# First mixer pass of a sandwich layer: x loaded ahead, the first of two row sums on GpSimd, the sums ahead of the scan, u by ScalarE

## What is computed

```python
x = x + 0.5 * _L0_ffn_ref(_layernorm(x, axis=-1), Wg, W11, W12, W2)      # 8 experts, 2 chosen per row
x = x + _L0_attn_ref(_layernorm(x, axis=-1), ...)                        # the mixer
x = x + 0.5 * _L0_ffn_ref(_layernorm(x, axis=-1), Wg, W11, W12, W2)
```

```python
rms = jnp.sqrt(jnp.mean(T * T, axis=-1, keepdims=True) + EPS)
x, z = jnp.split(T / rms * norm_scale @ in_w.T + in_b, 2, axis=-1)
gate = jax.nn.sigmoid(z)
xc = conv over 3 rows of x, per channel, + dw_b;  xc = xc @ pw_w.T + pw_b
u = xc @ win.T                              # 64 states, once forward, once backward
h = h * Abar + u_t * Bbar;  y_t = h * C     # a scan along the 4096 rows
y = (y_f @ wout_f.T + y_b @ wout_b.T) * gate
return T + y @ out_w.T + out_b
```

## Time and profile before

| | us |
|---|---|
| median of three runs (1027.65 to 1031.73) | 1029.53 |
| the profiled execution, by the clock of the runs | 1027.42 |
| its span in the profile | 1025.7 |
| TensorE busy in the span | 913.5 (89%) |
| VectorE busy | 603.9 (59%) |
| GpSimd busy | 547.1 (53%) |
| ScalarE busy | 356.7 (35%) |
| the first mixer pass lies at about | 431 to 546 |

### The profile page before, as it was taken

The page is one execution under the profiler, slowest core; times in us unless marked ns, Lnnn a source line. Parts: engine busy times, 40 slices in busy tenths (PEclk is TensorE's granted clock), DMA queues, the critical chain, the costliest instruction groups (busy, mean ns, idle before and its releaser), DMA issues.

```text
span 1025.7 us, 19076 instructions
## 1 busy us (share of the span) xinstructions
PE 913.5 (89%) x5386; PEld 784.5 (76%) x5390; DVE 603.9 (59%) x1456; ACT 356.7 (35%) x684; POOL 547.1 (53%) x565
## 2 busy tenths in 40 slices
PE   7669999999999999847787994599999999999994
PEld 7658888888888888726665784488888888888883
DVE  3976566565575655555655884755555555555552
ACT  3644344344343333223324531033333333333331
POOL 3435566565665555223212540166777677777762
PEclk9989999999999999958899995699999999999998
DMA  9653534525525421266511558133343333333322
GB/s 315 209 164 119 196 104 144 194 84 162 178 74 197 137 85 48 80 200 223 165 61 61 185 174 343 48 79 73 52 77 77 51 72 58 75 72 56 56 42 27
DMA packets 83903, 123.58 MB, mean 120 GB/s; under 512 B 12656, under 2 KB 64496, under 8 KB 83600
## 3 DMA queue, kind: packets, MB, share of 16 engines
q1 hardware_dynamic: 45344, 59.98, 17.6%
q0 software_dynamic: 24992, 37.32, 16.7%
q10 hardware_dynamic: 13520, 25.70, 7.5%
HBM read 74.67 MB, written 48.30 MB: 120 GB/s over the span
## 4 chain that ended last, share of the span: by engine, by line
PE 64%; DVE 14%; issue 8%; DMA 4%; POOL 4%; ACT 3%; ACTq 1%; another core or an unknown queue 1%; SPq 0%; POOLq 0%; DVEq 0%
PE bank L1493 34%; PE bank L1516 18%; PE bank L1502 5%; PE bank L1485 3%; DMA seq<-y_rows 2%; PE bank L1614 1%; DMA seq<-xt 1%; DVE bnst L878 1%; DVE work L1223 1%; POOL rstd L475 1%; POOL seq L502 1%; DVE work L1221 1%; DVE w_lo L1231 1%; ACT work L771 1%
## 5 line engine op out<-in xcount | busy, mean ns | idle before, releaser
L1163 DVE TENSOR_TENSOR sg<-sg,bank 128x512 f32<-128x512 f32 x142 | 97.7, 688 | 278.3 <-ACT sg L700 199.9
L1493 PE MATMUL bank<-w_hi,xt_hi 128*128 x568 | 238.0, 419 | 10.7 <-DVE xt_lo L1152 9.6
L1493 PE MATMUL bank<-w_hi,xt_lo 128*128 x568 | 223.8, 394 | 0.0
L1493 PE MATMUL bank<-w_lo,xt_hi 128*128 x568 | 223.5, 394 | 0.0
L511 POOL DMA_INDIRECT xg<-xn_rows,idx_i x142 | 140.5, 989 | 100.0 <-DVE idx_i L1001 42.0
L692 ACT ACTIVATE yb<-bank,gates_in 128x256 f32<-128x256 f32 x142 | 67.5, 475 | 306.6 <-PE bank L1516 257.6
L1516 PE MATMUL bank<-w_hi,ft_hi 128*128 x568 | 160.2, 282 | 2.2 <-ACT yb L692 2.2
L515 POOL DMA_INDIRECT gates_in<-gate_rows,idx_g x142 | 135.9, 957 | 47.7 <-issue 42.7
L1516 PE MATMUL bank<-w_lo,ft_hi 128*128 x568 | 160.4, 282 | 0.0
L1516 PE MATMUL bank<-w_hi,ft_lo 128*128 x568 | 160.2, 282 | 0.0
L525 POOL DMA_INDIRECT out_rows<-yb,idx_i x71 | 115.0, 1620 | 61.8 <-ACT yb L692 27.9
(11 more groups left out here) (268 smaller groups left out, 1256.5 us busy)
## 6 DMA issues: line engine op xcount, KB each, us to landing
w_lo_rows<-w_lo ACTq DMA_DIRECT2D x16, 512.0 KB
w_lo<-w_lo_rows SPq DMA_DIRECT2D x16, 512.0 KB
w_lo<-w_lo_rows SPq DMA_DIRECT2D x2, 4096.0 KB, 17.3
xn_rows<-work SPq DMA_DIRECT2D x14, 512.0 KB, 3.1
x_all<-x SPq DMA_DIRECT2D x8, 512.0 KB, 10.2
w_lo_rows<-in_sb ACTq DMA_DIRECT2D x16, 256.0 KB
work<-x SPq DMA_DIRECT2D x8, 512.0 KB, 3.4
states<-y_rows SPq DMA_DIRECT2D x8, 512.0 KB, 4.2
```

The source lines that it names most:

```text
L1163: nc.vector.tensor_tensor(sg[p], sg[p], ps_g[p][:], ALU.mult).then_inc(f_step, 1)
L1493: last = nc.tensor.matmul(dst[p][:], xt[p][:, c, :], of(w), start=(c == 0 and n == 0), stop=(c == DC - 1 and n == len(parts) - 1))
```

## The change

It has these parts, all in the first mixer pass:

1. x is not loaded chunk by chunk into `xin`. All of it goes to `x_place`, the places of `gate` where the gates of the same chunk will be written later: twelve half chunks as soon as the experts' weights have left that memory, the other four after the mixer's folded matrices are ready.
2. y has three buffer pairs, in `seq` and in `states` with `in_sb`. y of chunks 0 and 1 is loaded at once, y of chunk 2 after the matrices, and y of chunk i+2 when chunk i is summed (i from 1).
3. GpSimd adds the second choice's rows to the first (`sum_choices`), one chunk ahead of its `rsqrt_rms`. VectorE adds x and that sum, one addition where there were two.
4. VectorE does the sums and statistics of chunk c+4 ahead of the scan of chunk c.
5. u is taken by ScalarE (with a bias column `UBIAS` made beforehand), between the high parts and the gates.
6. The loops of ScalarE and VectorE are written out; zeros for the edge columns come from another place; TensorE's first filler matmuls wait for the first sum instead of the first x.

```diff
         xn_x = [xn[0], xn[1], states[:].rearrange("p a n -> p (a n)").rearrange("p (t d) -> p t d", d=D)]
-        y_in_sb = [states[:].rearrange("p a n -> p (a n)"), seq[:, 0, 3080:3080 + G * D]]
+        x_place = [gate[:, :, k * CH:(k + 1) * CH] for k in range(NCH)]
+        y_place = [[seq[:, 0, 8:8 + G * D], seq[:, 0, 8 + G * D:8 + 2 * G * D]],
+                   [seq[:, 0, 8 + 2 * G * D:8 + 3 * G * D], seq[:, 0, 8 + 3 * G * D:8 + 4 * G * D]],
+                   [states[:].rearrange("p a n -> p (a n)"), in_sb[:].rearrange("p a n -> p (a n)")]]
+        y_buffer = [0, 1, 2, 1, 2, 1, 2, 1]
...
+            sp.wait_ge(lo_out, 32 * E)
+            for i in range(NCH):
+                for h in range(2 if i < NCH // 2 else 1):
+                    load_x(i, h, x_early)
             for p in range(2):
                 sp.wait_ge(y_out[p], 16 * ((ET + 1 - p) // 2))
-            sp.wait_ge(lo_out, 32 * E)
-            load_x1(0, 0)
             load_y(0)
-            load_x1(1, 1)
+            load_y(1)
+            sp.wait_ge(m_ready, 1)
+            load_y(2)
+            for i in range(NCH // 2, NCH):
+                load_x(i, 1, x_late)
             for i in range(NCH):
                 b = i % 2
                 sp.wait_ge(summed, i + 1)
-                if i + 1 < NCH:
-                    load_y(i + 1)
+                if 1 <= i < NCH - 2:
+                    load_y(i + 2)
                 sp.dma_start(rows(x1_dram, i), xin[b]).then_inc(x1_out[b], 16)
-                if i + 2 < NCH:
-                    sp.wait_ge(norm_ready, i + 1)
-                    sp.wait_ge(x1_out[b], 16 * (i // 2 + 1))
-                    load_x1(i + 2, b)
...
+            def sum_choices(i):
+
+                first, second = y_place[y_buffer[i]]
+                pool.wait_ge(y_in[y_buffer[i]], 32 * y_buffer[0:i + 1].count(y_buffer[i]))
+                nc.gpsimd.tensor_tensor(first, first, second, ALU.add).then_inc(half_sum, 1)
+
+            sum_choices(0)
             for i in range(NCH):
+                if i + 1 < NCH:
+                    sum_choices(i + 1)
                 rsqrt_rms(i, i % 2)
...
+            def take_u(c, b):
+
+                act.wait_ge(u_done, c + 1)
+                if c >= NCH // 2:
+                    act.wait_ge(summed, NCH)
+                nc.scalar.activation(seq[:, 0, c * CH + 1:(c + 1) * CH + 1], ps_u1[b][:], ACT.Identity, scale=ssm[:, BBAR:BBAR + 1], bias=ssm[:, UBIAS:UBIAS + 1]).then_inc(u_ready, 1)
...
+            def stats_x1(i, b):
+                x_rows, y_rows = x_place[i], y_place[y_buffer[i]]
...
+                if i >= 2:
+                    dve.wait_ge(x1_out[b], 16 * (i // 2))
+                    dve.wait_ge(norm_ready, i - 1)
                 dve.wait_ge(half_sum, i + 1)
-                nc.vector.tensor_tensor(flat, flat, y_in_sb[1], ALU.add).then_inc(summed, 1)
+                halves = lambda a: a.rearrange("p (h n) -> p h n", h=2)
+                whole_ = xin[b].rearrange("p t d -> p (t d)")
+                nc.vector.tensor_tensor(halves(whole_), x_rows, halves(y_rows[0]), ALU.add).then_inc(summed, 1)
                 dve.wait_ge(summed, i + 1)
                 ln_stats(i + NCH, b, rows_of(b))
```

More of the change, by code:

```diff
@@ L262, in build @@
         xn_x_out = [sem(f"xn_x_out{b}") for b in range(3)]
+        y_in = [sem(f"y_in{b}") for b in range(3)]
         y_out = [sem(f"y_out{b}") for b in range(2)]
-        y_in, half_sum, summed, norm_dve, norm_act, r_ready = (sem(n) for n in ("y_in", "half_sum", "summed", "norm_dve", "norm_act", "r_ready"))
+        x_early, x_late, half_sum, summed, norm_dve, norm_act, r_ready = (sem(n) for n in ("x_early", "x_late", "half_sum", "summed", "norm_dve", "norm_act", "r_ready"))
         x_in = [sem(f"x_in{b}") for b in range(2)]
@@ L780, in _ @@
             norm_x1(3, 1)
-            with act.Fori(0, NCH // 2 - 2) as j:
-                for b in range(2):
-                    rows_high(j * 2 + (b + 2), b)
-                    gate_out(j * 2 + (b + 1))
-                    norm_x1(j * 2 + (b + 4), b)
-            for i in range(NCH - 2, NCH):
-                rows_high(i, i % 2)
-                gate_out(i - 1)
-            gate_out(NCH - 1)
+            for c in range(NCH):
+                if c + 2 < NCH:
+                    rows_high(c + 2, c % 2)
+                take_u(c, c % 2)
+                if c + 1 < NCH:
+                    gate_out(c + 1)
+                if c + 4 < NCH:
+                    norm_x1(c + 4, c % 2)
             def take_states(i, b, c):
@@ L1286, in _ @@
             for b in range(2):
-                stats_x1(b, 0, b)
+                stats_x1(b, b)
             dve.wait_ge(m_ready, 1)
@@ L1290, in _ @@
             rows_low(0, 0)
-            stats_x1(2, 1, 0)
+            stats_x1(2, 0)
             rows_low(1, 1)
-            stats_x1(3, 1, 1)
-            with dve.Fori(0, NCH // 2 - 2) as j:
-                for b in range(2):
-                    c = j * 2 + b
-                    take_u(c, b)
-                    rows_low(j * 2 + (b + 2), b)
-                    scan_forward(c)
-                    stats_x1(j * 2 + (b + 4), j + 2, b)
-            nc.vector.memset(states[N:P, 1, 0:1], 0.0).then_inc(bwd_done, 1)
-            for c in range(NCH - 4, NCH):
-                take_u(c, c % 2)
-                if c < NCH - 2:
-                    rows_low(c + 2, c % 2, last=(c == NCH - 3))
-                scan_forward(c)
+            stats_x1(3, 1)
+            for c in range(NCH):
+                if c + 2 < NCH:
+                    rows_low(c + 2, c % 2, last=(c == NCH - 3))
+                if c + 4 < NCH:
+                    stats_x1(c + 4, c % 2)
+                scan_forward(c)
+            nc.vector.memset(states[N:P, 1, 0:1], 0.0).then_inc(bwd_done, 1)
             def scan_backward(i, b):
@@ L1635, in _ @@
             pe.wait_ge(m_ready, 1)
-            pe.wait_ge(x_in[0], 16)
+            pe.wait_ge(summed, 1)
             keep_busy(ps_t1[1][0][:], before.unsqueeze(1).to_broadcast([P, G, P]), 12)
```

35 lines of the change are left out of this document (17 added, 18 removed).

## The result

The changed kernel takes 1023.66 us in the median of eleven runs (1018.82 to 1026.26), the kernel before 1029.53 (1026.92 to 1032.83). The ratio is 0.9939, with a 95% interval of 0.9922 to 0.9956: 6.3 us less by it (4.5 to 8.0), 5.9 by the medians. The prediction was 1024.2. The profiled execution of the changed kernel has a span of 1022.1 us against 1025.7, 3.6 less.

What follows compares the result with a forecast made beforehand. The first pass was taken to be bound by a loop of latencies among VectorE, GpSimd and ScalarE, no engine full. Start -3.2, three loops -4.1 and end +2.05 gave -5.3 us: 1024.2 from 1029.53, range 1021 to 1028.

Steps and rivals of the forecast that it cites:

- The loop: Steady chunk of the first pass: falls from 12.36 to 10.98 us, 1.38 less.
- The scan's 1.19 and the add's 1.23: Steady chunk: moving the scan and giving one add to GpSimd take 1.19 and 1.23 us off VectorE's chain.
- The block: Steady chunk: the scan, now beside GpSimd's small rstd steps, holds them up and costs 1.04 us.
- The rival in which GpSimd gets through: Steady chunk: scan does not hold GpSimd up, loop 9.94 us, total -11.0, 1018.5 us; chance 0.15.
- The start: First chunks of the pass: low halves of chunk 2 come 1.8 us earlier, of chunk 3 3.2 us.
- TensorE's first product: Start: u of chunk 0 ready at 472.3 us; evacuation of chunk 2 waits for it, low halves follow at 473.4.
- x ahead: Start: early x loads cost nothing, and y of chunk 0, first in the queue, comes 1.4 us earlier.
- The end: Hand-over to the second pass: last u, scan and two hand-offs stand before the states' copy, 2.05 us more.
- The sum: Whole kernel: -3.2 start, -4.1 chunks 4 to 6, +2.05 end, -5.3 us; median 1024.2 us.
- the start gains nothing and new meetings of adds take half of each loop's gain: Start and steady chunks: only -0.8 us in total, 1028.8 us; chance 0.20.
- the rival of the late load: Steady chunk: y landing after 7.3 us makes GpSimd's sum delay VectorE's add; up to +4.3, 1033.8 us; chance 0.06.
- TensorE at half clock in the whole pass: First pass: clock sinks to 1.2 GHz, TensorE becomes the loop, +20 us with the end, 1049 us; chance 0.04.

Runs made afterwards that it cites:

- scan behind rstd: Changed kernel, with the scans of chunks 0 to 3 also waiting for GpSimd's rstd; ratio to the kernel before 0.9900.
- last kernel: Changed kernel with u before gates, scan behind rstd, first product ahead of chunk 2's transposes, ten fillers, and both adds of chunks 0 and 1 on VectorE; ratio 0.9823.
- kernel of the mends and fillers: Changed kernel with u before gates, scan behind rstd, first product ahead of chunk 2's transposes, and ten filler products behind the last gates; ratio 0.9835.
- product first kernel: Changed kernel, with TensorE's 36 products for u of chunk 0 ahead of the transposes of chunk 2; ratio to the kernel before 0.9918.
- u before gates: Changed kernel, with ScalarE taking u of the last chunk ahead of the last chunk's gates; ratio to the kernel before 0.9906.
- u on VectorE: Changed kernel with one part undone: VectorE takes u again, ahead of the low halves; ratio to the kernel before 0.9903.

## Why the prediction was right

**The loop.** Forecast 10.98, measured 10.82. The scan's 1.19 and the add's 1.23 left it as written. The block was sized at 1.04 from the earlier trace rows and measured 0.87: the first step took 1.10, and it had been 0.23, not 0.20. Undoing one part each gave 12.08 (add back) and 9.96 (block away), and moving the scan alone in the kernel before gave 12.08 instead of 12.37, which is 1.19 off and 0.90 back. So all three terms are shown.

**The block by the scan.** The rival in which GpSimd gets through is refuted by the scan behind rstd: same scan, same GpSimd steps, other place. The rule of the Trainium skill (SBUF — State Buffer, "Who interferes with whom"), that a VectorE instruction with two inputs in SBUF and a GpSimd instruction that reads SBUF exclude each other, holds in these runs for adds too where VectorE is first: 1.13 us at 442.95, 1.10 and 1.25 in the last kernel, and each of these steps ends within 0.1 us of the add beside it.

Where GpSimd is first, the runs show two cases. Behind a long sum VectorE pays, as in the kernel of the mends and fillers, where a scan that met two sums took 3.20 us instead of 1.28:

```profile
532.88 4.77 POOL L511 TENSOR_TENSOR seq<-seq,outb_sb 128x1024 f32<-128x1024 f32 x2 [25.97 <-ACT seq L830]
...
535.54 3.20 DVE L1337 TENSOR_TENSOR_SCAN states<-ssm,states 64x512 f32<-64x512 f32 x1
```

Beside a small step that had begun it does not: VectorE's add at 442.80 came behind a GpSimd step of 442.75 and took its usual 1.23 us, the step its usual 0.23. With the scan behind rstd the same holds for the scan, which began at 486.29 beside a GpSimd step of 1.01 us that had begun at 486.20, and took 1.28. So that edit found a place for the scan where neither engine pays; what in a small step leaves VectorE free is not shown.

**The start.** Forecast 1.8 us at chunk 2 and 3.2 at chunk 3; measured 1.6 and 3.16. From M the gains are 2.1 and 3.7; half a microsecond went ahead of M, part of it a longer chain of small steps there. In the forecast TensorE's first product was the last link, and the product first kernel shows that it was. That the sum came out so close is partly luck, for two links behind each other are off and nearly cancel: the transposes of chunk 2 began at 464.24 and not 465.1, and from them to the low halves it took 9.35 us at a granted clock of 0.70, where 8.3 had been put. In kernels alike up to there the same stretch took 8.28 us at 0.79, and chunk 2 came 1.1 us earlier. x ahead was costed at 1.4 us for the first chunk and won 1.45, counted from the first load behind the experts.

**The end.** Forecast +2.05, measured +2.28 (2.87 less 0.59): ScalarE took 0.77 us for u where 0.65 had been taken from its nearest rows, which is 0.12 of the 0.23, and the rest is hand-offs. The kernels that take the last u elsewhere (u before gates, u on VectorE) have it back at 0.58 and 0.59.

**The sum.** By the states' copy the changed kernel was 5.54 us ahead (546.36 to 540.82), against a forecast of 5.3: 3.16 at the start (3.2), 4.65 in the three loops (4.1), 2.29 lost at the end (2.05). Behind it the two profiles differ by what the forecast had not: TensorE's idle time at the hand-over grew from 2.67 to 4.97 us, its clock stayed at 1.2 GHz for 10.2 us instead of 3.4, and VectorE's first sum of the second pass was only 3.56 us ahead (557.28 to 553.72). This term of 2.0 us was missing, and the spans confirm it: 1022.1 against 1025.7, 3.6 less. That the medians lie 5.9 apart, at the forecast, is therefore luck in part. The profiled execution of the kernel before was 2.1 us faster than its median and that of the changed kernel 0.2 us slower, and this is the difference between 3.6 and 5.9. What makes the executions of one kernel differ by this much is not shown. The stretch at low clock is a candidate (3.4 us in one kernel with the same gap), and so is TensorE's clock in the pass; how often the changed kernel meets the long stretch was not measured.

**The other rivals.** The one in which the start gains nothing and new meetings of adds take half of each loop's gain is out by the 1.6 us at the start and the loop of 10.82. y landed in 5.2 us (median, at most 7.0), so it never came in the way of an add in the loop, and the rival of the late load did not decide; its limit of 7.3 was closer than I had put it. TensorE at half clock in the whole pass did not occur; its clock was 1.00 in three of the four loops and 0.84 in the other.

## What to carry to other kernels

When work moves to an idle engine or an instruction changes place, look at which instructions now start together: the scan on VectorE, put beside GpSimd's small steps, gave back 0.87 of the 1.19 us that its move had won, and one wait that sent it into idle time won them again. Read the last pass through each queue by itself, for a step that is free in the loop can stand alone at the end (here 2.3 us for one u). Where an engine's clock falls behind idle time, a gap can cost more than its length. Fillers in it kept the clock up in three of three profiles; one kernel with them was 3.4 us faster, with overlapping intervals, and the other showed no gain in time.
